# A factorization-machine network on one core: arrays of four factors, three copied and one left in PSUM, and quarter interaction blocks

## The reference

```python
e = stack([tbl_f[ids[:, f]] for f in range(39)], axis=1)      # 512 x 39 x 16
X0 = Xi = e
for W in (W0, W1):                      # (39*39, 128), (39*128, 128)
    z = einsum('bmd,bnd->bdmn', X0, Xi).reshape(b, d, -1)
    Xi = einsum('bdp,po->bod', z, W)
    res.append(Xi)
z = sum(concatenate(res, axis=1), axis=-1)                    # 512 x 256
h = relu(concatenate([z, dense_ctx], 1) @ W_top1 + b_top1)    # 512
h = relu(h @ W_top2 + b_top2)                                 # 256
y = h @ W_top3
```

## Time and profile before

| | us |
|---|---|
| three runs of the kernel | 230.61 median, 230.29 to 232.42 |
| the profiled execution's own time | 230.19 |
| its span, first to last instruction | 228.6 |

### The profile page before, as it was taken

How to read it: one execution, slowest core, us unless ns; L and a number is a source line. 1 busy time by engine, 2 the same in 40 slices (tenths; PEclk the granted TensorE clock), 3 DMA queues, 4 the chain that set the end, 5 groups by cost and what they waited for, 6 DMA issues and landing times.

```text
span 228.6 us, 4760 instructions
## 1 busy us (share of the span) xinstructions
PE 204.9 (90%) x1715; PEld 156.0 (68%) x1715; DVE 176.5 (77%) x295; ACT 167.6 (73%) x300; POOL 109.2 (48%) x106
## 2 busy tenths in 40 slices
PE   4577956879989998999999899799999999999995
PEld 4577813435556566777787577577778888889794
DVE  0899956999869899999979998798899787532010
ACT  6999465769867999798879998697867575775003
POOL 4788777777777777877777778000000000000000
PEclk9999779999999999999999999999999999999999
DMA  5950000240392591200240000003100000000000
GB/s 143 217 128 7 9 7 6 65 69 6 77 236 66 70 314 29 44 5 7 65 65 7 7 7 7 1 3 94 22 3 0 0 3 0 1 0 3 0 0 3
DMA packets 22015, 10.26 MB, mean 45 GB/s; under 512 B 11576, under 2 KB 20877, under 8 KB 21992
## 3 DMA queue, kind: packets, MB, share of 16 engines
q1 hardware_dynamic: 18728, 9.11, 16.4%
q0 software_dynamic: 3264, 0.84, 3.9%
HBM read 8.63 MB, written 1.31 MB: 44 GB/s over the span
## 4 chain that ended last, share of the span: by engine, by line
PE 60%; DVE 17%; ACT 9%; issue 7%; DMA 4%; POOL 1%; SPq 1%; DVEq 0%; ACTq 0%
PE s_bank L1013 14%; PE side_bank L967 6%; PE side_bank L969 6%; PE side_bank L968 6%; PE g_bank L995 4%; DVE z L786 3%; DVE z_lo L796 3%; DVE w_sb L725 3%; PE b_bank L947 3%; PE side_bank L962 3%; PE side_bank L995 3%; PE side_bank L934 3%; PE side_bank L975 2%; DMA feat<-tbl,ids_sb 2%; PE side_bank L912 2%
## 5 line engine op out<-in xcount | busy, mean ns | idle before, releaser
L387 POOL DMA_INDIRECT feat<-tbl,ids_sb x102 | 109.0, 1069 | 33.3 <-issue 21.9
L575 ACT ACTIVATE z_hi<-z 128x512 fp32r<-128x512 f32 x100 | 61.9, 632 | 10.6 <-DVE z L786 8.7
L786 DVE TENSOR_TENSOR z<-factors,b_bank 128x512 f32<-128x512 f32 x84 | 57.1, 681 | 7.9 <-PE b_bank L947 3.7
L796 DVE TENSOR_TENSOR z_lo<-z,z_hi 128x512 fp32r<-128x512 f32 x84 | 57.8, 688 | 0.3 <-ACT z_hi L575 0.2
L1013 PE MATMUL s_bank<-g,w_sb 128*128 128x128 f32 x312 | 47.5, 279 | 0.0
L1013 PEld LDWEIGHTS s_bank<-g,w_sb 128*128 128x128 f32 x312 | 44.1, 192 | 4.8 <-issue 2.4
L967 PE MATMUL side_bank<-z_hi,w_hi 128*128 128x512 f32 x84 | 42.3, 504 | 0.0
L969 PE MATMUL side_bank<-z_hi,w_lo 128*128 128x512 f32 x84 | 33.2, 396 | 0.0
L968 PE MATMUL side_bank<-z_lo,w_hi 128*128 128x512 f32 x84 | 32.9, 392 | 0.0
L467 ACT ACTIVATE factors<-side_bank 128x512 f32<-128x512 f32 x31 | 18.4, 594 | 7.2 <-PE side_bank L934 7.2
L947 PE MATMUL b_bank<-xs,sel 117*128 117x512 bf16 x48 | 18.7, 389 | 1.4 <-DVE direct_z L786 0.8
(11 more groups left out here) (181 smaller groups left out, 333.0 us busy)
## 6 DMA issues: line engine op xcount, KB each, us to landing
w_sb<-w SPq DMA_DIRECT2D x3, 832.0 KB, 5.8
feat<-tbl,ids_sb POOLq DMA_INDIRECT x102, 2.4
lines<-line SPq DMA_DIRECT2D x4, 320.0 KB, 2.2
diag<-lines SPq DMA_DIRECT2D x32, 40.0 KB
wt_sb<-wt SPq DMA_DIRECT2D x2, 512.0 KB
g<-small SPq DMA_DIRECT2D x1, 770.0 KB
g<-small SPq DMA_DIRECT2D x1, 448.0 KB
w0p<-w_pair SPq DMA_DIRECT2D x1, 448.0 KB
```

Of the source, the lines that this page charges most:

```text
L387: nc.gpsimd.indirect_dma_start(feat[:, bt % 2, n * D:(n + 1) * D], None, tables[order[n]], bass.IndirectOffsetOnAxis(ids_sb[:, bt, n:n + 1 ...
L575: nc.scalar.activation(z_hi[:, s % RING, :], z[:, at, :], ACT.Copy).then_inc(rounded, 1)
L786: nc.vector.tensor_tensor(target, one, other, ALU.mult).then_inc(product, 1)
L796: nc.vector.tensor_sub(low[rows, s % RING, :], z[rows, SPLITS[s] % Z_RING, :], z_hi[rows, s % RING, :].bitcast(f32)).then_inc(remainder, 1)
```

## The change

- **Arrays.** Three arrays a, b and c are copied to `factors` (with two chunks' room instead of three), and one array stays in PSUM. The six products of different arrays are ab, ac, bc, ad, bd, cd, in this order, then aa. The tables `BASES` and `CHAIN` that lay pairs on partitions are replaced (`FOURS`, `THREES`); weights are laid out accordingly on the host.
- **Banks.** a and c are filled in `b_bank[1]`, b in `turn_bank`; the array that stays is in `b_bank[0]`, selected once in a chunk (`SELECT_AT`). The two halves of the turned features go to the two banks, both at step 24 (tile 0: 21 and 24).
- **Interaction blocks.** Four bands of 32 rows with 80 columns: 16 matmuls in a chunk, each band in a bank of its own. ACT copies the pair in `side_bank` first.
- **Steps.** `TURN_XI` and with it `G_AT` come one step later; layer 2 still starts at the same step.
- **DMAs.** The three pieces of W1 are issued by SP ahead of its loop over chunks, when tile 0's features are turned, the dense weights at chunk 1. The pacing of the gathers begins with the 40th.

```diff
-SELECTS = 3
-BASES = ((0, 5, 10, 13, 20), (0, 14, 3, 16, 21), (0, 8, 12, 14, 17))
-CHAIN = (1, 3, 0, 2, 4)
-LEAD = 2
+COPIES = "abc"
+ARRAYS = len(COPIES) + 1
+ORDER = ((0, 1), (0, 2), (1, 2), (0, 3), (1, 3), (2, 3), (0, 0))
+SELECT_AT = 1
...
-F_RING = 3
+F_RING = 2
...
-PACED_FROM = 33
-W1_AT = [3, 3, 4]
-MLP_IN = 5
+PACED_FROM = 40
+MLP_IN = 1
...
-TURN_XI = COPY_XI + 2
+TURN_XI = COPY_XI + 3
 G_AT = TURN_XI + 2
-BANDS = 2
+BANDS = 4
...
-FILL_A = 4
-FILL_B = 3
+FILL_AT = (2, 4, 5)
...
-X_AT = [[], [21, 23], [23, 24], [23, 24]]
-A_AT = [0, 24, 25, 25]
-B_AT = [0, 25, 26, 26]
-S2_AT = SPT - PT + G_AT + 3
+X_AT = [[], [21, 24], [24, 24], [24, 24]]
+NEXT_FILL_AT = [(), (25, 26, 26), (25, 26, 26), (25, 26, 26)]
+S2_AT = SPT - PT + G_AT + 2
...
-        turn_banks = [turn_bank, g_banks[1], l1_bank[1], b_bank[1][:]]
+        turn_banks = [turn_bank, b_bank[1][:], g_banks[1], l1_bank[0], l1_bank[1]]
...
+            sp.wait_ge(*after(turn_filled, "x", 0, XJ - 1))
+            for k in range(W1_PIECES):
+                m = slice(k * F // W1_PIECES, (k + 1) * F // W1_PIECES)
+                sp.dma_start(w1_sb[:, m, :], w1.rearrange("(m n) o -> n m o", n=O)[:, m, :]).then_inc(w1_in, 16)
...
             take_factor("a", 0)
+            take_factor("c", 0)
...
-                k, j = u % 2, u // 2
-                if u < 2:
-                    dve.wait_ge(*after(turn_taken, "ab"[u], i, 0))
-                one = factors[:, i % F_RING, k, :]
-                if u == REST_T:
-                    other = one
-                else:
-                    dve.wait_ge(selected, SELECTS * i + j + 1)
-                    other = b_bank[(SELECTS * i + j) % B_RING][:]
+                for k, name in enumerate(COPIES):
+                    if u == max(k - 1, 0):
+                        dve.wait_ge(*after(turn_taken, name, i, 0))
+                if u == len(COPIES):
+                    dve.wait_ge(selected, i + 1)
+                one, other = (factors[:, i % F_RING, k, :] if k < len(COPIES) else b_bank[0][:] for k in ORDER[u])
                 nc.vector.tensor_tensor(target, one, other, ALU.mult).then_inc(product, 1)
...
-                        to = [*g_banks, *side][BANDS * (r // SET_SUBS) + h]
+                        to = [*side, *g_banks][BANDS * (r // SET_SUBS) + h]
```

More of the change, by code:

```diff
@@ L49 @@
 LAG = 5
-B_RING = 2
 DIRECT = [[1, 3, 5], [], [], []]
@@ L1205, in _factors @@
         for t in range(REST_T):
[L1206 to L1209 removed]
+            if max(ORDER[t]) < len(row):
+                item = tuple(sorted(row[k] for k in ORDER[t]))
+                if item not in seen:
+                    seen.add(item)
+                    pairs[t, p] = item
     for at in base_at:
```

165 lines of the change are left out of this document (86 added, 79 removed), and 3 rows, old and new, of the table FOURS.

## The result

The changed kernel takes **234.9 us** (median of four executions: 233.1, 234.4, 235.4 and 244.7) against 230.5 for the kernel before; the ratio is 1.018, with a 95% interval of 1.014 to 1.023. It is 1.8% slower, where 6% was forecast. Ratios are made from the executions of each kernel that lie within 1.5% of its fastest, so the 244.7 is not in this one; where a kernel's executions scatter, their whole range stands beside.

What follows compares the result with a forecast made beforehand. POOL's stream of gathers was taken to set the time until the last lands, PE in tile 3. Sum: 230.2 + 17 - 2.9 + 0.3 = 244.6, forecast 245.0 us, 6% slower; range 236 to 257, at 70%.

Steps and rivals of the forecast that it cites:

- Part 1: DVE's products: longer runs of instructions with two SBUF operands hold POOL's gathers, so the last is issued 17 us later.
- one hand-over in five opens: Rate at which a waiting gather gets in between two such DVE instructions; 2.3 us lost for each chunk instead of 3.55.
- undisturbed stream: POOL's gathers at 1.25 us from start to start, without holds; the last would be issued at 133.7.
- closed or nearly closed one: Gather stream if no hand-over opens (31.9 us lost, last gather 165.6) or one in five does (18.1, 151.8).
- Rival 2: Waiting gathers get in at every second hand-over; a chunk loses about 0.5 us, +2.9 in all, 233 us; chance 9%.
- rival 1: A gather waits for one DVE instruction at most; stream ends near 142, only part 3 counts, 227.6 us; chance 13%.
- Part 2: DVE's waits for late features at the splits are part of the 17; behind them PE, ACT and layer 1 run dry.
- slow restart: PE would stand several us at the splits where its clock was full; counted only in the range 236 to 257.
- Part 3: PE behind the last gather: fewer selections or fills -0.9, five four-band interaction blocks -1.0, turned features -1.0; together -2.9 us.
- The turned features: PE's 1.90 us stand before turning tile 3's features shrinks, first copy going to the needed bank; -1.0, at most -1.9.
- Part 4: ACT's 16 more copies, 9.5 us, mostly hidden; up to 0.6 may show once after the last gather, taken as +0.3.
- Part 5: Banks, DMAs and steps: alternating banks 0, pacing 0, early W1 loads 0 (at worst +1), blocks a step later no change.

Runs made afterwards that it cites:

- i2: Changed kernel, all six pair products reading the selected array in PSUM (wrong pairs), selection one step earlier; 229.5 to 232.3 us, ratio 1.000.
- h1: Changed kernel with one added wait: POOL issues the very last gather only when layer 1 has used 74 steps; 235.0 and 239.2 us.
- h2: Changed kernel, last gather held until layer 1 used 74 steps, ACT's xit copy ahead of the split's pieces; 239.0 and 239.9 us, ratio 1.037.
- h4: Changed kernel, last gather held until layer 1 used 74 steps, 14 unread matmuls on PE before chunk 9's interaction block; 238.4 and 245.1 us.
- i1: Changed kernel, products ordered ab, ad, ac, bd, bc, cd, aa, d selected one step earlier; median of eleven 233.0 us, ratio 1.003 from the first five.
- h3: Kernel before, with the very last gather held until layer 1 has used 74 steps; 237.2 us twice, ratio 1.027.
- i3: Kernel before, every product the square of its own SBUF factor copy (pairs left out); 228.8 to 232.0 us (6), 235.5 to 236.9 (3), ratio 0.996.
- e2: Kernel before, every product the square of its own SBUF factor copy (pairs left out), in a run with stops; 253.3 us, ratio 0.992.
- e, f and g runs: Ten runs, of the changed kernel or variants of either kernel, with unexplained stops; the kernel before took 253 to 256 us there (medians).
- e4: Changed kernel, products ordered ab, ad, ac, bd, bc, cd, aa, d selected one step earlier, in a run with stops; ratio 1.027.
- h runs: Four runs without stops, of both kernels, all with an added wait that makes the last gather late; kernel before without it 231.0 us.

## Why the prediction was wrong in size

In short, the profiled span is 2.9 us longer: 3.7 for the last gather, 1.0 for a second copy and 1.6 for the lower clock behind it, less 3.5 that PE gained.

- **The bound** (POOL's gathers set the time until the last one lands): right. DVE waits there again, 3.50 us, and removing the SBUF partners (i2) removes the loss.
- **Part 1, "17 us later": the failed step.** The hold exists, the end of the run plus 0.82 us as forecast, and a long run does it (3.20 us at 142.01, the same once in h1 and in h2). What failed is the count behind it, "one hand-over in five opens", taken from five gathers of one trace, four of them long ones, which are those that had been passed over. In the changed kernel's profile 32 of the 77 gathers took over 1.0 us. Together they were passed over at 5 hand-overs; 15 of them got in at one, the other 17 at the end of a run or at a gap, and 11 more started on a hand-over and took 0.94. Of the waiting gathers, then, three in four get in at a hand-over; counted alike it is 14 of 20 in h1, but only 15 of 25 in h2, 13 of 25 in h4 and 12 of 22 in i1. So a chunk loses some tenths, now and then 2 to 3 us, instead of 2.3 to 3.6 each time. In the forecast's own sum the undisturbed stream ends at 133.7 and the closed or nearly closed one 31.9 or 18.1 us behind it; the excess was 12.1, and the last gather came 3.7 us later than before, not 17. Rival 2 (every second hand-over opens, 233) was nearest in time, and in h4 and i1 in its rate as well. The forecast also gave every hand-over the same chance, whatever the gather's phase, and the trace of before had the counter-evidence: the median gather took 0.946 with remainders all around, which I gave rival 1 as its point and left at 13%.
- **Part 2, behind DVE's wait everything runs dry**: right, and with a price that was left out of the sum. PE stood for 3.15 us and its clock fell to 1.2 GHz for 6.8, which cost 1.6 us; h3 shows the kernel before paying 2.4 us when its gather is late. The forecast named a slow restart for its range only.
- **Part 3, "-2.9"** (with part 4's +0.3: -2.6 from landing to end): right in sum at the full clock, by other terms. 84.4 us before; 81.9 in h4 and in i1, both with a clock of 1.00 in the stretch behind the landing, which is -2.5 (i2, which waits for its selection, has 82.9). In the first profile it is 83.6, -0.8: the lower clock took the difference back. Behind the first product it is 3.5 us less (h1, h2, h4 and i1 have 72.4 to 72.5). Counted on PE, the blocks there give 1.4 (six, where five were forecast), selections and fills, 13 instead of 18, 1.2, and 0.9 is work of the two layers that now stands ahead of the first product. The turned features did not gain their 1.0 (a's copy ends 8.3 behind the landing as before).
- **Part 4, +0.3**: mis-sized. The copy of b delays the first product by 1.04 us, but PE uses 0.9 of it for the work named above, so little of it is left in the sum.
- **Part 5, loads and pacing 0**: no run undid them alone. The idle time between gathers is the same 23.2 us in both first profiles, so the pacing held none and freed none; i2 contains both and is level with the kernel before, so in sum they cost at most what part 3 gives, 2.5 us.
- **Signs.** Gathers of 2.5 to 4 us: yes, but two, not one a chunk. Last gather near 159: 145.5. DVE idle before `rest` for 15 us: 5.7. The forecast's sign of being wrong (longest gather near 2 us, last one before 145) did not show, at 3.20 and 145.5, though the time was 10 us off: it told the forecast from rival 1, but not frequent holds from rare ones. Tile 3 in 38 us: 36.45. Interaction block at most 1.3: 1.13.

The Trainium skill, SBUF — State Buffer, "Who interferes with whom", infers that a tensor_tensor with two SBUF inputs leaves DMAs that GpSimd issues alone. The rows of 3.20 and 8.02 us speak against it, and the times of i3 show how it can look true: in step, the hold costs 0.05 us of DVE's time.

## What to carry to other kernels

A contention between two periodic streams can't be priced by its worst case times the number of meetings: look first whether they fall into step, by listing all meetings and not only the long ones, and be ready for the cost to differ from execution to execution. Where one engine's wait leaves PE idle for some microseconds, add the lower clock behind it to the sum, for the kernel before too if its wait gets longer, and ask which work it will fall on. And a part that gains behind a bound that wanders by 1 to 3 us, as the bands do, may be there in the trace and still not be measurable.

## What the runs showed of the hardware beyond that

- A gather can be held 8.0 us by back-to-back DVE instructions with two SBUF operands (e2), while in the same trace others pass at each second hand-over in 0.94. What decides whether a hand-over lets a waiting gather in stays open.
- DVE pays for a gather that it lets in: 0.73 instead of 0.68 us for the product that starts with it.
- With four bands of 32 rows, four loads of 128 columns start within 0.01 us and the next four 0.11 later; at the lower clock the block takes 2.01 us instead of 1.13.
- 3.4 us at 1.2 GHz cost 0.4 us of the way to the first product in h1 and 1.0 in h2, by what PE had to do in them.
- The e, f and g runs took 10% longer for every kernel (255 against 231 us), with waits of up to 12.6 us (e4) that nothing in the profile explains. Their chips had the numbers 0, 1 and 7, and that of the h runs, which have no such waits, the number 1 again, so it stays open whether the chip is the cause. The changed kernel's ratio there (1.024) agrees with 1.018 within its interval, although POOL's gathers were not waited for at the end; what makes it slower there was not found.
